# Score bursts of six, six and four heads, the gate rectified by ScalarE, part of a feed-forward moved a pass later, and new engine orders, in a two-block transformer kernel on Trainium2

## The reference

```python
def layer(x, cond, mask):
    # conditioning: top-2 of 8 routed experts of width 64 and two shared ones
    p = _leaky(x @ sw_gate) * (x @ sw_up) @ sw_down        # _leaky: v if v >= 0 else 0.01 * v
    y = sum_top2(weight_e * (_leaky(x @ w_gate[e]) * (x @ w_up[e])) @ w_down[e]) + p
    # banded causal linear attention without softmax
    q, k, v = split(y @ W_qkv + b_qkv)
    x = x + layer_norm(((q @ k.T / scale) * band) @ v) * ln_w + ln_b
    # attention, 16 heads of 64, one shared key and value head, null key and value
    xn = ln(x, g_norm); q = l2norm(xn @ Wq) * q_scale; k = l2norm(xn @ Wk) * k_scale
    sim = q @ k.T * 8 + bias[h, i - j]          # 128 x 129 a head and sequence
    z = ln(softmax(masked(sim)) @ v @ Wout, g_out)
    # feed-forward 128 -> 512 -> 512 -> 512 -> 128
    h = silu(z @ w1 * s1) * (z @ w2 * s2)
    h = gelu(h @ h1 * s3); h = gelu(h @ h2 * s4)
    return x + h @ w3 * s5
```

## Time and profile before

| | |
|---|---|
| median of 3 runs | 865.01 us |
| the profiled execution | 863.99 us |
| its span, first to last instruction | 861.9 us |
| TensorE busy | 806.7 us (94%) |
| VectorE busy | 605.4 us (70%) |
| ScalarE busy | 617.3 us (72%) |
| GpSimd busy | 453.8 us (53%) |
| mean granted TensorE clock | 0.990 |

### The profile page before, as it was taken

How to read it: one execution, slowest core, us unless ns; L and a number is a source line. 1 busy time by engine, 2 the same in 40 slices (tenths; PEclk the granted TensorE clock), 3 DMA queues, 4 the chain that set the end, 5 groups by cost and what they waited for, 6 DMA issues and landing times. The chain is left out here.

```text
span 861.9 us, 16913 instructions
## 1 busy us (share of the span) xinstructions
PE 806.7 (94%) x5368; PEld 604.3 (70%) x5368; DVE 605.4 (70%) x1621; ACT 617.3 (72%) x1660; POOL 453.8 (53%) x388
## 2 busy tenths in 40 slices
PE   4988989999999999999999999999999999799987
PEld 3765566677766778577766768577776777577877
DVE  5878898967678666967668676876668676665522
ACT  2425776589748987498857987499856897498854
POOL 3128767754573565554584374645665365863210
PEclk9999999999999999999999999999999999799999
DMA  7041100000100001000010001000010000000000
GB/s 242 1 129 60 50 2 29 1 1 1 30 12 2 1 1 42 1 2 1 1 41 1 2 1 41 1 2 1 1 41 1 2 2 14 1 1 1 14 6 7
DMA packets 15589, 16.99 MB, mean 20 GB/s; under 512 B 1408, under 2 KB 13072, under 8 KB 15120
## 3 DMA queue, kind: packets, MB, share of 16 engines
q1 hardware_dynamic: 15504, 15.92, 5.8%
HBM read 13.81 MB, written 2.11 MB: 18 GB/s over the span
## 5 line engine op out<-in xcount | busy, mean ns | idle before, releaser
L605 POOL TENSOR_TENSOR sb_sm<-sb_sm,sb_rden 128x512 f32<-128x512 f32 x128 | 135.8, 1064 | 253.4 <-DVE sb_rden L1070 252.8
L699 ACT ACTIVATE sb_sm<-sb_sm,sb_nmx 128x129 f32<-128x129 f32 x512 | 199.1, 393 | 25.9 <-DVE sb_nmx L1065 24.3
L598 POOL TENSOR_TENSOR sb_biasm<-sb_bias,sb_maskn 128x512 f32<-128x512 f32 x128 | 164.8, 1301 | 13.7 <-issue 5.7
L1057 DVE SCALAR_TENSOR_TENSOR sb_sm<-ps_S,sb_rq,sb_biasm 128x129 f32<-128x129 f32 x512 | 143.5, 343 | 37.7 <-PE ps_S L1289 29.5
L1289 PEld LDWEIGHTS ps_S<-sb_k,sb_qs 64*128 64x128 f32 x1024 | 69.2, 189 | 58.5 <-issue 56.9
L1289 PE MATMUL ps_S<-sb_k,sb_qs 64*128 64x129 f32 x1024 | 93.2, 300 | 15.0 <-DVE sb_sm L1057 14.2
L588 POOL TENSOR_TENSOR sb_rq<-sb_qss,sb_mhalf 128x16 f32<-128x16 f32 x32 | 93.2, 2936 | 16.3 <-DVE sb_qss L1043 16.3
L699 ACT ACTIVATION_READ_ACCUMULATOR sb_sm<-sb_sm,sb_nmx 128x1 f32 x512 | 96.9, 189 | 0.0
L706 ACT ACTIVATE sb_pT<-ps_T 128x512 f32<-128x512 f32 x128 | 74.8, 592 | 26.4 <-PE ps_T L1297 26.4
L1065 DVE TENSOR_REDUCE sb_nmx<-sb_sm 128x4 f32<-128x516 f32 x128 | 86.0, 678 | 0.8
L1297 PE MATMUL ps_T<-sb_ident,sb_sm 128*128 128x128 f32 x512 | 79.3, 279 | 4.2 <-POOL sb_sm L605 3.6
(11 more groups left out here) (227 smaller groups left out, 1806.4 us busy)
## 6 DMA issues: line engine op xcount, KB each, us to landing
sb_xg<-in_xT SPq DMA_DIRECT2D x8, 256.0 KB, 3.9
sb_xs<-in_x SPq DMA_DIRECT2D x8, 256.0 KB, 4.3
sb_qs<-in_xT SPq DMA_DIRECT2D x1, 2048.0 KB, 10.6
sb_hA<-in_h SPq DMA_DIRECT2D x2, 1024.0 KB, 4.9
out_y<-sb_res SPq DMA_DIRECT2D x7, 256.0 KB, 2.4
sb_sm<-toeplitz SPq DMA_DIRECT2D x1, 1024.0 KB, 5.8
sb_rows<-in_rows SPq DMA_DIRECT2D x1, 648.0 KB, 6.4
sb_oT<-in_wq SPq DMA_DIRECT2D x1, 512.0 KB, 10.4
```

Of the source, the lines that this page charges most:

```text
L598: pool.tensor_tensor(biasm[:, heads, 1:NK], bias0[:, heads], maskn[:, j // 4].unsqueeze(1).broadcast_to([128, 4, S]), ALU.add)\
L605: pool.tensor_tensor(sm[:, heads, 1:NK], sm[:, heads, 1:NK], rden[:, heads].unsqueeze(2).broadcast_to([128, 4, S]), ALU.mult)\
L699: ins = act.activation(sm[:, h], sm[:, h], ACT.Exp, bias=nmx[:, h:h + 1], accum_out=den[:, h:h + 1])
L1057: ins = dve.scalar_tensor_tensor(sm[:, h], bank(g, "sim", j, odd)[:, m * NK:(m + 1) * NK], rq[:, k * HEADS + h:k * HEADS + h + 1], biasm[: ...
```

## The change

1. `sim` and `score` work on bursts of 6, 6 and 4 heads of a row (`BURSTS`, in pairs of heads), three heads or two to a bank, so 12 steps a group and not 16. The steps that go by four heads wait for the burst that holds their last head (`LAST_BURST`).
2. The gate's copy on ScalarE becomes a Prelu with slope 0.01; VectorE's instruction at L913 and its semaphore go.
3. The last two l3 steps and the l4 of group 5 (stage E) move from the seventh pass to the beginning of the last one. The seventh pass has an order of its own for that.
4. The two expert weights are fetched from ScalarE's queue, `wd` earlier on SyncE's.
5. All orders are written anew.

```diff
+BURSTS = ((0, 3), (3, 6), (6, 8))
+NB = len(BURSTS)
+LAST_BURST = (0, 1, 1, 2)
...
     "pe steady": """
...
+        sim.0 rw.0 exp.0-1 sim.1 exp.2-3 sim.2 exp.4 down.0 PT.0 sim.3 zT.0 PT.1 qkv.0 l1.0 sim.4 l1.1 PT.2 l1.2
+        PT.3 PV.0-1 l1.3 sim.5 scores.0 z.0 l2.0-1 PT.4 sim.6 l2.2 PT.5-6 l2.3 mix.0 sim.7 l3.0-1 PT.7 l3.2
+        sim.8 PV.2-3 sim.9 z.1 PT.8 xnT.0 l3.3 PT.9 kv.0 q.0 PT.10 sim.10 q.1 z.2-3 q.2 PT.11 sim.11 PV.4-5
+        qs.0-1 q.3 PT.12 q.4 z.4 q.5 PT.13 l4.0 q.6 PV.6 PT.14 qs.2-4 q.7 kT.0 PT.15 z.5 qs.5-7 PV.7 qst.0 z.6-7
...
     "pe last": """
...
+        sim.0 l3p.2 sim.1 l3p.3 sim.2 l4p.0 PT.0 zT.0 sim.3 PT.1 l1.0-1 sim.4 PT.2 l1.2-3 PV.0 sim.5 PT.3 l2.0-1
...
     "act steady": """
...
+        xh.0 rw.0 exp.0-3 ex.0 exp.4 ex.1-3 down.0 zT.0 qkv.0 l1.0 PT.0 h1.0 PT.1 l1.1 PT.2 h1.1 PT.3 l1.2 PV.0
...
     "dve fill": """
...
+        exp.4 rt.7 down.0 rt.8 maskn.0 qkv.0 scores.0 xl.0 pl.1 mix.0 pl.2 ln1.0 rt.9 ln2.0 xnT.0 q.0-2 kv.0
...
+LATE = {step + "p": step for step in ("l3", "l4")}
+STAGE |= {step: "E" for step in LATE}
+PART |= LATE
...
-PHASES = {-1: "fill", 0: "start", NG - 1: "last", NG: "drain"}
+PHASES = {-1: "fill", 0: "start", NG - 2: "seventh", NG - 1: "last", NG: "drain"}
...
-            shift = {"P": 1, "A": 1, "B": 0, "C": -1, "D": 0}[STAGE[step]]
+            shift = {"P": 1, "A": 1, "B": 0, "C": -1, "D": 0, "E": -2}[STAGE[step]]
...
+            act.dma_start(wgu_raw[:, 0], a["wg"]).then_inc(load["wg"], 16)
+            act.dma_start(wgu_raw[:, 1], a["wu"]).then_inc(load["wu"], 16)
...
-                act.activation(gs[:, c % 2], bank(g, "exp", c, 0)[:], ACT.Copy).then_inc(gate_copied.sem, 1)
+                act.activation(gs[:, c % 2], bank(g, "exp", c, 0)[:], ACT.Prelu, alpha=0.01).then_inc(gate_leaked.sem, 1)
...
-                dve.wait_ge(gate_copied.sem, gate_copied.at(g, c + 1))
-                dve.scalar_tensor_tensor(gs[:, c % 2], gs[:, c % 2], 0.01, gs[:, c % 2], ALU.mult, ALU.max)\
-                    .then_inc(leaked.sem, 1)
+                dve.wait_ge(gate_leaked.sem, gate_leaked.at(g, c + 1))
...
-            def score(g, j):
+            def score(g, n):
+                k, (lo, hi) = n // NB, BURSTS[n % NB]
+                last = (2 * hi - 1) // 4
                 dve.wait_ge(q_rnorm.sem, q_rnorm.at(g, k + 1))
-                dve.wait_ge(bias_ready.sem, bias_ready.at(g, j + 1))
-                dve.wait_ge(pt_psum.sem, pt_psum.at(g, j - 3))
+                dve.wait_ge(bias_ready.sem, bias_ready.at(g, 4 * k + last + 1))
+                dve.wait_ge(pt_psum.sem, pt_psum.at(g, 4 * (k - 1) + last + 1))
                 for odd in range(2):
-                    dve.wait_ge(sim_psum.sem, sim_psum.at(g, 2 * j + odd + 1))
-                    for m in range(2):
+                    dve.wait_ge(sim_psum.sem, sim_psum.at(g, 2 * n + odd + 1))
+                    for m in range(hi - lo):
...
-            def sim(g, j):
-                k = j // 4
-                ps = [free(g, "sim", j, odd, (kT_copied, 1), (q_copied, NP)) for odd in range(2)]
-                for m in range(2):
+            def sim(g, n):
+                k, (lo, hi) = n // NB, BURSTS[n % NB]
+                ps = [free(g, "sim", n, odd, (kT_copied, 1), (q_copied, NP)) for odd in range(2)]
+                for m in range(hi - lo):
```

More of the change, by code:

```diff
@@ L51 @@
     "pe fill": """
[L52 to L55, removed]
+        lg.0 warm.0-2 pb.0-1 warm.3-7 lg.1-2 rw.0 exp.0 lg.3-4 exp.1 lg.5 exp.2 lg.6-7 pb.2 warm.8 exp.3-4
+        warm.9 down.0 pb.3 warm.10-12 qkv.0 scores.0 warm.13 mix.0 warm.14 fl.0 warm.15 fl.1-2 warm.16 xnT.0
@@ L56 @@
+        fl.3 q.0-2 warm.17 kv.0 q.3 qs.0-1 q.4-5 qs.2-3 q.6 qs.4 q.7 qs.5-7 warm.18 qst.0 warm.19-21 kT.0
     """,
     "pe start": """
[L58 to L61, removed]
+        rw.0 sim.0 exp.0 sim.1 exp.1 sim.2 exp.2-3 PT.0 sim.3 PT.1 exp.4 PV.0 sim.4 PT.2 down.0 sim.5 PT.3 qkv.0
@@ L62 @@
+        scores.0 PV.1 mix.0 PT.4 sim.6 PT.5-6 sim.7 PV.2 z.0-1 PT.7 sim.8 z.2 sim.9 PT.8-9 xnT.0 PV.3 PT.10
+        sim.10 q.0-1 sim.11 kv.0 q.2 PT.11 q.3 PT.12 PV.4 qs.0-2 q.4-5 z.3 q.6 qs.3 PT.13 z.4 qs.4-5 PV.5-6 q.7
+        PT.14 kT.0 PT.15 qs.6 z.5 qs.7 PV.7 qst.0 z.6-7
     """,
     "pe steady": """
[L64 to L65 removed]
@@ new lines @@
+        qs.0-1 q.3 PT.12 q.4 z.4 q.5 PT.13 l4.0 q.6 PV.6 PT.14 qs.2-4 q.7 kT.0 PT.15 z.5 qs.5-7 PV.7 qst.0 z.6-7
+    """,
+    "pe seventh": """
+        rw.0 sim.0 exp.0-1 sim.1 exp.2-3 sim.2 exp.4 down.0 sim.3 zT.0 PT.0-1 qkv.0 PT.2 l1.0-1 PT.3 l1.2-3
+        sim.4 PV.0 scores.0 sim.5 PV.1 l2.0 sim.6 PT.4-5 z.0 PT.6 mix.0 sim.7 PV.2 l2.1 sim.8 l2.2 PT.7 z.1 l2.3
+        sim.9 PV.3 PT.8 xnT.0 l3.0 PT.9-10 kv.0 sim.10 l3.1 q.0 PT.11 q.1 sim.11 z.2 q.2 PV.4 q.3-4 z.3 qs.0-2
+        PT.12 q.5 PV.5 z.4 q.6-7 PT.13 qs.3-4 PT.14 qs.5 kT.0 z.5 PT.15 qs.6-7 PV.6 qst.0 PV.7 z.6-7
@@ new lines @@
+        inv.13 max.14 q.2-3 max.15 inv.14 q.4 kT.0 inv.15 q.5 l4.0 q.6 ssq.0 ssc.0 q.7 vs.0
+    """,
+    "dve seventh": """
+        rw.0 xl.0 ln3.0 sim.0 exp.0 max.0 exp.1 sim.1 exp.2 max.1 exp.3-4 inv.0 max.2 sim.2 max.3 inv.1-2 zT.0
+        down.0 zl.0 inv.3 qkv.0 sim.3 l1.0-1 h1.0 max.4 h1.1 l1.2-3 sim.4 max.5 h1.2 sim.5 h1.3 inv.4 scores.0
+        inv.5 max.6 inv.6 sim.6 max.7 sim.7 max.8 inv.7 mix.0 max.9 inv.8 h2.0 max.10 ln1.0 sim.8 h2.1 inv.9
+        ln2.0 max.11 h2.2 inv.10 h2.3 xnT.0 sim.9 max.12 kv.0 inv.11 sim.10 inv.12 maskn.0 q.0-1 max.13-14
+        sim.11 max.15 inv.13 q.2 kT.0 inv.14 q.3-4 inv.15 q.5-7 ssq.0 ssc.0 vs.0
```

138 lines of the change are left out of this document (69 added, 69 removed).

## The result

| | before | after |
|---|---|---|
| median | 865.51 us | 853.10 us |
| range (4 runs each) | 864.04 to 867.41 | 851.64 to 853.67 |
| span of the profiled execution | 861.9 | 851.9 |

The ratio is 0.9853, 95% interval 0.9829 to 0.9876: 12.4 us faster. The forecast was 21.5 less, 843. The direction and the range of 831 to 858 held; the gain is little over half of what was expected. The time lies outside the forecast's own 836 to 850, in the band that the prediction gave to rival (1). The profiled execution after is the slowest of its four (853.67), the one before took 863.99, so the spans differ by 10.0 us and the medians by 12.4.

A forecast was written before the change was run, and what follows sets the result against it. TensorE's queue length and gaps were taken to set the end (806.7 of 861.9 us busy). Terms -7 -7 -3.5 -7 +0 +3 = -21.5 gave 842.5, adjusted to 843.5 and rounded to 843 us; range 831 to 858.

The forecast's parts named there:

- rival (1): Expert-stage waits only move, to steps hanging on POOL and the norm: about 852 us (849 to 858), chance 0.22.
- Bursts, -7: Score bursts on TensorE: fewer bursts save 0.9 us a pass for 8 passes, -7 us (-3 to -12.8).
- Rival (2): Six-head bursts hold both score banks longer on VectorE, so TensorE waits: slower, up to 879 us, chance 0.08.
- the wait for the row before: Score steps: a score waits until up to two groups of the row before are transposed; given no separate size.
- the 0.56 us of the bank: Score banks: VectorE drains six heads, not four, 0.56 us longer; 36 us if met in all 64 long bursts.
- Gate, -7: Expert stage: VectorE loses 40 gate instructions; 1.2 us of TensorE's waits goes in six passes, -7 us (0 to -10).
- Rival (3): ScalarE gates: Prelu needs its own table, about 36 loads, 46 us of ScalarE; +22, 865 us, chance 0.05.
- Start pass, -3.5: Start pass: five fewer gates and three bursts for VectorE to drain among expert steps, -3.5 us (0 to -6).
- TensorE's five short waits: Start pass: TensorE waits for VectorE's drain of a score bank at five bursts, 3.4 us in all, 1.2 at most.
- Fill, 0 (-2 to +2.5): Fill: expert weights fetched from ScalarE's queue land things about 1 us earlier, against warm-ups, lg.1-2 and routing inside the norm.
- Late feed-forward, -7: Head of last pass: moved l3 and l4 steps, 9.2 us, cover idle or slow-clock time, -7 us (-3 to -9.5).
- New waits, +3: Shorter slack after transpose xnT and PV.7's copy ahead of z.7: 0.1 to 1 us a pass, +3 (0 to +8).

The follow-up runs named there:

- the gate alone: Kernel before, with ScalarE's gate copy made a Prelu and VectorE's leak left out, orders and bursts as before: 854.40 us, ratio 0.9861.
- The second run without them: Kernel after, l3.2, l3.3 and l4 of group 5 back in the seventh pass, which takes the middle passes' orders: 862.06 us.
- two of the experiments: Not named; apparently GpSimd held during the second norm in the kernel after (854.58 us), and two start-pass steps moved in the combined kernel (843.43, from 843.92).

## Why the prediction held in part

**Bursts, -7: right in the middle passes.** Between the gate alone and the whole change a middle pass goes from 97.4 to 96.2 and TensorE's busy time in it from 95.64 to 94.54, both at clock 1.00: 1.1 us against my 0.9. That the order of the other steps has no part in the 1.1 was not shown. The matmuls of the scores are busy 83.1 us, not 93.2, but some of that is the slow head of the last pass, where a burst took 1.23 us. Rival (2) did not come in the middle passes. It is real all the same: in an order not made for it the long burst cost 65 us, and the waits came from what I had put in half a sentence, the wait for the row before, and from the steps behind it on VectorE, not from the 0.56 us of the bank; a good quarter of the price was slow clock.

**Gate, -7: right in size, partly by luck, and short in reach.** 1.2 us a pass, as taken, though the waits for the gate that went were 0.6 and two of the waits I summed for it stayed; the rest came from a shorter bank wait and 0.4 less of busy time. By itself it gives 11.4, with 2.4 in the start pass; the 2.1 in the fill of its profile can't be told from scatter. Rival (3) is out: 66 loads, none at the gate, and 77 with the gate alone, as before.

**Start pass, -3.5: wrong in sign.** The step that failed is "VectorE has five gates less and three bursts to drain among the five expert steps". With its gates alone the start pass gained 2.4, two thirds of that term. The order with long bursts then lost 6.2 (71.1 to 77.3): TensorE is idle 4.0 us more and busy 2.2 us more, at a clock of 0.98 in place of 1.00. I took fewer bursts for less waiting and read TensorE's five short waits as the whole cost; VectorE's order of steps between them was never followed. The waits for banks are now four and 5.7 us. Of the 6.2 no run tells what is the bursts' length and what the order.

**Fill, 0 (-2 to +2.5): outside its bounds**, +4.2 in this pair of profiles, some 3.7 between the means of seven and six. I saw both delays, two warm-ups with lg.1-2 ahead of rw, and the routing inside the norm, and let an earlier load and the q copies pay for them. The loads paid nothing (the first step of all came 2.8 us later with them), the delays add up (1.8, 1.9), and kv's place behind three q steps, 1.1, I had not looked at.

**Late feed-forward, -7: right for the steps, wrong for the two passes.** The second run without them gives 9.0, and the clock at the head of the last pass is 1.00, as expected. But the seventh pass takes 89.9 and not about 87, and the last one 100.1, and the two together gain 6.3 and not 9.2: without the late steps the new last pass would have been 4.5 us longer than with short bursts (102.1 to 97.6), and for that loss the sum had no term.

**New waits, +3: the place was right, the reason was not.** The transpose of the second norm waits 1.6 us a pass, not for the slack behind it but for the norm ahead of it, which GpSimd holds up. A bound of 1 us a pass was too small. Rival (1), waits that only move, did not come for the gate; 853.10 lies in its band of 849 to 858 by chance. But it is what happened in two of the experiments.

So the forecast fell short by its first 155 us, and the range held because it had room for that. The gate gives 11.4 by itself. From the kernel with the gate alone to the whole change, the profiles gain 6.1 in the five middle passes and 5.1 in the last two, and lose 12.5 by the end of the start pass (142.7 to 155.2) and 0.5 in the drain: 1.8 longer in the two profiled spans, 1.3 shorter in the medians, so nothing that these runs tell from zero.

## What to carry to other kernels

Try the smallest part of a change alone first: here one function on ScalarE gave nearly all of the gain, and the rest of the change lost as much at the beginning as it won later. A longer step on an in-order queue is paid by what stands behind it and by what it waits for ahead, so price it at its place in the queue of the engine that drains it, in every stage, the short ones too. When a wait is removed and the period stays, look at what the freed engine meets next: a step that waits for someone else may stand ahead of the one that is needed, and moving it back costs nothing. And before a stage's length in one profile is put down to an edit, compare the granted clock and the same stage in the other profiles.
